# Gates behind the experts instead of in front, two experts at a time on 64 rows each, and a new order of the stages

## The chip, the core and the metric

The kernel runs on one core of a Trainium2 chip. The core has four engines that matter here: TensorE (PE, matrix products into PSUM; its weight loads are listed as PEld), VectorE (DVE), ScalarE (ACT) and GpSimd (POOL); SyncE (SP) issues the transfers. Each engine works its own instructions in program order and waits at semaphores for the others. The metric is the device time of one execution in microseconds (us), lower is better. All data are fp32.

## What is computed

The input x has 4 sequences of 4096 rows of 512. Every row goes through a mixture-of-experts network, every second row through a recurrence, and both are multiplied and added to x:

```python
xn = _layernorm(x)
# recurrence on every second row, state h of 512 x 64 per sequence
h = jnp.tanh(h * A + xt[:, :, None] * Bm);  y = h @ c_sum + Dv * xt
s = repeat(einsum(y * silu(gate), w_out) + b_out, 2)
# experts, E = 8, top 2 of 8, EH = 512, M = 64
cont = sigmoid(xn @ W_enc + b_enc) @ W_s2c + b_s2c
gate = top-2 softmax weights of cont @ Wr + br
he = relu(einsum('tm,emh->eth', cont, W1) + b1[:, None, :])
y = einsum('eth,ehm->etm', he, W2) + b2[:, None, :]
expert_out = einsum('etm,te->tm', y, gate)
g = silu(layernorm(sigmoid(expert_out @ W_c2s + b_c2s) @ W_dec + b_dec))
out = x + s * g
```

The gates are not negative. So an expert can be weighted on its input and biases (relu(g(Wc + b)) = g relu(Wc + b)) or on its output.

## The kernel before

**Blocks and steps.** The time axis is cut into 64 blocks of 32 recurrence steps. The four sequences and a half of the 64 states fill the 128 partitions; the other half of the states is a second tile, f = 1. One step is, for f = 0 and 1: VectorE multiplies h by A (`ps_z`, L1138), adds u (L1144), and ACT takes the tanh into a ring of 8 buffers `h` (L598). The order on VectorE is multiply 0, multiply 1, add 0, add 1. POOL makes u = x * B for a step (L525). PE reads four steps of h out at a time (`y`, L887, 16 instructions of 32 columns in four column groups, into `ps_y`); the tanh of every fourth step waits until the readout of the steps 8 to 5 before it is done, since it overwrites their buffers.

**The network beside it.** While block n recurs, the 256 rows of a block (two tiles q of 128) pass through: input normalisation, transposes and projection (`proj_...`), `encode`, `controller` (cont, transposed: contT), `router`, six small `route` steps and `route_gate` on VectorE, the experts, `to_spikes`, `decode`, an output layernorm (`dec_scale`, `dec_shift` on VectorE), and a last stage that joins both branches (`fin_...`). PSUM has two banks, `bank0` and `bank1`, for all of this, and `ps_acc`. A bank is filled by PE, drained by another engine, and filled again.

**The experts before.** ACT weights cont by each gate (`scale_cont`, L705 and L707, one copy of 64 columns for each expert and tile, with the gate as a 65th column), PE transposes the results (`conteT_transpose`, L959), ACT copies them (L718), and `expert_up` (L973) multiplies 65 rows, the last being the bias b1 against the gate. One call fills one bank for one half of an expert. ACT takes the relu of 512 columns (L724), `expert_down` (L985) adds 64 output rows on either half of the columns into `ps_acc`, all experts into one sum, with b2 against the transposed gates (L949, L981). `eo_fold` adds the halves (L1004). The readout is copied by ACT (`fin_y`, L666) and multiplied with the silu gate by POOL (`fin_gate`, L558).

**What sets the order.** Each engine runs the same loop over blocks in slots of a sixteenth of a step. Tables of constants at the head of the file say in which slot of its block a stage is issued on an engine: 19.9375 is behind the last instruction of step 19, numbers over 32 lie in the next block, negative ones in the one before. On VectorE the second multiply of a step is at .25 and the adds at .5 and .75; on ACT the second tanh is at .5. On PE the slots are only an order, since PE has no instruction of its own in a step. The functions `experts`, `y` and all others are called from these tables.

Of the kernel before, what the change touches and what calls it, by code (L numbers as in the profile page):

```python
# [51 lines left out]
EARLY = 16 * 12  # L52
LATE = 16 * 9
# [13 lines left out]
POOL_PROJ_SCALE = -23.875  # L70
POOL_DEC_SCALE = (31.8125, 34.6875)
POOL_FIN_SKIP = 0.4375
POOL_FIN_GATE = 36.3125
POOL_FIN_ADD = (43.375, 59.1875)
ACT_PROJ_NORM = -23.4375
ACT_PROJ_EVAC = (-22.6875, -20.25)
ACT_PROJ_SEED = (-22.3125, -9.125)
ACT_PROJ_OUT = (-20.4375, -7.25)
ACT_FIN_Y = 33.8125
ACT_Y_SEED = 5.625  # L80
ACT_SPIKES = (2.9375, 3.8125, 4.6875, 5.875)
ACT_CONTT_COPY = 6.8125
ACT_ROUTE_SIG = 9.5
ACT_SCALE_CONT = (9.9375, 10.625)
ACT_CONTET_COPY = (12.625, 12.75, 12.75, 12.9375)
ACT_GATET_COPY = 11.6875
ACT_RELU = (13.375, 13.875, 14.5625, 14.75, 15.5, 15.5625, 16.5625, 16.5625, 17.8125, 17.8125, 18.8125, 20.9375, 21.625, 21.875, 22.6875, 22.8125)
ACT_EO_COPY = 23.625
ACT_BOTH_COPY = 24.875
ACT_SPIKES_AGAIN = (25.75, 25.9375, 26.625, 27.75)  # L90
ACT_DEC_SILU = (31.5, 39.9375)
ACT_DEC_SQUARE = (29.9375, 31.625)
ACT_PROJ_SUM = (-29.25, -29.0625)
ACT_PROJ_MEAN = -28.9375
ACT_PROJ_SQUARE = (-28.0625, -27.375)
ACT_PROJ_VAR = -25.0625
ACT_FIN_EVAC = 39.875
ACT_ACC_SEED = 5.625
ACT_OUT_SEED = 38.9375
ACT_DEC_SEED = (26.3125, 27.875)  # L100
PE_Y = (19.1875, 20.375, 21.5, 34.8125, 34.9375, 37.25, 38.125, 38.375)
PE_PROJ_TRANSPOSE = (-12.0, -10.625)
PE_PROJ_IN = (-11.5625, 4.625)
PE_ENCODE = (6.4375, 7.1875, 7.3125, 11.1875)
PE_CONTROLLER = 17.125
PE_ROUTER = 19.0625
PE_CONTET = (22.0, 26.3125, 27.4375, 28.0)
PE_GATET = 21.4375
PE_EXPERTS = (28.9375, 33.3125, 34.0, 34.125, 34.4375, 34.4375, 35.5625, 35.9375, 36.25)
PE_EO_FOLD = 36.75  # L110
PE_TO_SPIKES = (36.9375, 37.3125)
PE_DECODE = (37.4375, 37.8125)
PE_FIN_TRANSPOSE = 50.8125
PE_FIN_OUT = 51.25
DVE_ROUTE = (7.75, 8.75, 9.375, 9.5, 9.625, 9.75)
DVE_ROUTE_GATE = 10.0
DVE_DEC_SCALE = (31.625, 35.8125)
DVE_DEC_SHIFT = (31.8125, 37.9375)
DVE_FIN_MUL = 42.875


def build(nc, x, w_inT, b_in, A_T, B_T, Cm, Dv, w_outT, b_out, g_norm, W_enc, b_enc, W_s2c, b_s2c,
# [12 lines left out]
    with ExitStack() as ctx:  # L135
# [17 lines left out]
        w_1 = sb("w_1", [P, E, EH])  # L153
# [6 lines left out]
        ones = sb("ones", [P, P])  # L160
# [29 lines left out]
        conte = sb("conte", [P, 2, E, MA])  # L190
        hT = sb("hT", [P, 2, 2 * T2])
# [1094 lines left out]
```

## Time and profile before

| | us |
|---|---|
| median of 3 runs | 5803.53 (5802.18 to 5803.68) |
| span of the profiled execution | 5801.0 |
| PE busy | 5580.6 |
| VectorE busy | 5403.5 |
| POOL busy | 5287.9 |
| ACT busy | 4595.4 |

The profiled execution is 2.5 us shorter than the median of the runs. Busy times count overlapped instructions once. A row of the timeline merges equal instructions that follow one another: start, time from the first start to the last end, engine, line, operation, output<-inputs, shapes, count, and in brackets the idle time before it and what ended it. Two instructions in a row on an engine overlap by their tail, so what one holds the engine is the distance of two starts, less than its own duration.

### The profile page before, as it was taken

To read this page: it belongs to the slowest core of one execution; us is meant where nothing else is said; L and a number is where in the kernel's file an instruction comes from. 1 tells how busy PE (TensorE), PEld (TensorE's weight loads), DVE (VectorE), ACT (ScalarE), POOL (GpSimd) and SP (SyncE) were. 2 spreads that over 40 slices of the span, in tenths; PEclk is the share of its full clock that TensorE was granted. 3 is DMA by queue.
4 is the path that set the end of the run, shared out by engine and by line. 5 is a ranking of instruction groups with operands and counts; after the bars stand their busy time and mean duration, and the time that the engine had idled before them with its cause. 6 is when DMAs were issued, how large, how long until landed. Compare 5 with 4: busy or idle time off the path is not lost.

```text
span 5801.0 us, 88242 instructions
## 1 busy us (share of the span) xinstructions
PE 5580.6 (96%) x28770; PEld 3073.1 (53%) x28770; DVE 5403.5 (93%) x9108; ACT 4595.4 (79%) x9941; POOL 5287.9 (91%) x2828
## 2 busy tenths in 40 slices
PE   6999999999999999999999999999999999999998
PEld 3555555555555555555555555555555555555554
DVE  5999999999999999999999999999999999999997
ACT  5878878788788787887887878878878788788786
POOL 5999999999999999999999999999999999999997
PEclk9999999999999999999999999999999999999999
DMA  6454544544444445444454454444444444444443
GB/s 166 113 121 107 122 115 111 123 112 116 120 108 121 116 111 122 112 116 120 108 120 117 110 121 113 115 120 109 119 118 110 120 114 114 120 110 118 119 109 88
DMA packets 158222, 673.41 MB, mean 116 GB/s; under 512 B 45761, under 2 KB 46785, under 8 KB 92225
## 3 DMA queue, kind: packets, MB, share of 16 engines
q1 hardware_dynamic: 157762, 667.76, 48.0%
q8 instruction: 229, 3.75, 0.3%
q14 instruction: 231, 1.89, 0.1%
HBM read 617.26 MB, written 50.33 MB: 115 GB/s over the span
## 4 chain that ended last, share of the span: by engine, by line
PE 76%; ACT 14%; DVE 7%; issue 3%; SPq 1%; DMA 0%; POOL 0%; ACTq 0%; POOLq 0%
PE bank L973 17%; PE bank L921 15%; PE ps_y L887 11%; PE ps_acc L985 9%; PE bank L1037 8%; PE ps_acc L1037 8%; ACT h L598 4%; PE bank L908 4%; DVE ps_z L1144 4%; ACT conte L707 3%; DVE ps_z L1138 2%; ACT wide L718 1%; PE bank L1020 1%; PE ps_acc L1020 1%; PE bank L959 1%
## 5 line engine op out<-in xcount | busy, mean ns | idle before, releaser
L525 POOL TENSOR_TENSOR u<-xb,bt 128x1024 f32<-128x1024 f32 x2048 | 4811.0, 2360 | 387.1 <-DVE ps_z L1144 315.6
L598 ACT ACTIVATE h<-ps_z 128x512 f32<-128x512 f32 x4096 | 2408.0, 599 | 1008.3 <-DVE ps_z L1144 807.9
L1138 DVE TENSOR_TENSOR ps_z<-h,ps_A 128x512 f32<-128x512 f32 x4096 | 2664.7, 691 | 314.7 <-ACT h L598 233.1
L1144 DVE TENSOR_TENSOR ps_z<-ps_z,u 128x512 f32<-128x512 f32 x4096 | 2655.3, 691 | 0.0
L973 PE MATMUL bank<-wide,w 65*128 65x256 f32 x4096 | 1015.0, 393 | 18.5 <-ACT wide L718 18.5
L887 PE MATMUL ps_y<-h,c_wide 128*32 128x512 f32 x8192 | 962.0, 599 | 49.0 <-ACT h L598 49.0
L921 PE MATMUL bank<-xnT,w_enc 128*128 128x256 f32 x4096 | 901.3, 381 | 2.8 <-ACT wide L671 2.8
L973 PEld LDWEIGHTS bank<-wide,w 65*128 65x128 f32 x4096 | 730.6, 189 | 315.3 <-issue 152.6
L921 PEld LDWEIGHTS bank<-xnT,w_enc 128*128 128x128 f32 x4096 | 772.9, 190 | 158.9 <-issue 53.3
L887 PEld LDWEIGHTS ps_y<-h,c_wide 128*32 128x32 f32 x8192 | 227.2, 109 | 566.8 <-issue 418.1
L908 PE MATMUL bank<-w_in,xnT 128*128 128x512 f32 x1024 | 474.4, 606 | 7.6 <-DVE c_wide L1214 1.6
L1037 PE MATMUL bank<-w_dec,wide 128*128 128x512 f32 x1024 | 456.6, 599 | 0.0
L1037 PE MATMUL ps_acc<-w_dec,wide 128*128 128x512 f32 x1024 | 449.9, 592 | 0.0
L908 PEld LDWEIGHTS bank<-w_in,xnT 128*128 128x128 f32 x1024 | 185.0, 190 | 274.0 <-issue 272.0
L1037 PEld LDWEIGHTS ps_acc<-w_dec,wide 128*128 128x128 f32 x1024 | 194.6, 190 | 244.9 <-issue 244.9
L724 ACT ACTIVATE hT<-bank 128x512 f32<-128x512 f32 x512 | 291.9, 599 | 37.3 <-PE bank L973 37.2
L1037 PEld LDWEIGHTS bank<-w_dec,wide 128*128 128x128 f32 x1024 | 189.3, 190 | 235.5 <-issue 214.6
L724 ACT ACTIVATE conte<-bank 128x512 f32<-128x512 f32 x512 | 291.2, 598 | 24.3 <-PE bank L973 24.3
L985 PE MATMUL ps_acc<-hT,w 128*64 128x256 f32 x2048 | 277.5, 392 | 0.0
L985 PE MATMUL ps_acc<-conte,w 128*64 128x256 f32 x2048 | 274.3, 389 | 0.0
L1057 PE MATMUL bank<-w_out,conte 128*128 128x512 f32 x512 | 238.5, 609 | 8.4 <-ACT conte L769 0.7
L707 ACT ACTIVATE conte<-ps_acc,gate 128x64 f32<-128x64 f32 x1024 | 228.5, 384 | 0.0
(124 smaller groups left out, 4285.1 us busy)
## 6 DMA issues: line engine op xcount, KB each, us to landing
xb<-x_proj_scratch SPq DMA_DIRECT2D x2048, 256.0 KB, 4.6
xbuf<-in_L_attn_x SPq DMA_DIRECT2D x256, 128.0 KB
xres<-in_L_attn_x SPq DMA_DIRECT2D x512, 64.0 KB
out<-g SPq DMA_DIRECT2D x256, 128.0 KB
x_proj_scratch<-xp SPq DMA_DIRECT2D x256, 64.0 KB
w_in<-in_L_attn_w_in SPq DMA_DIRECT2D x1, 2048.0 KB, 8.1
w_enc<-in_L_ffn_W_enc SPq DMA_DIRECT2D x1, 2048.0 KB, 16.5
w_dec<-in_L_ffn_W_dec SPq DMA_DIRECT2D x1, 2048.0 KB, 20.4
```

What stands on the lines that cost most here:

```text
L525: pool.tensor_tensor(u[:, tau % 2, :, :], xt, bt[:, :, :], ALU.mult).then_inc(u_ready, 1)
L598: act.activation(h[:, tau % RING, f, :], ps_z[:, f, :], ACT.Tanh).then_inc(h_ready, 1)
L707: ins = act.activation(conte[:, q, e, 0:M], cont_acc[:, q, :], ACT.Copy, scale=gate[:, q, e:e + 1])
L724: drained(act.activation(hidden[n % 4], bank[n % 2][:, :], ACT.Relu), at)
L887: ins = pe.matmul(ps_y[32 * j:32 * j + 32, :], c_wide[:, f, SP - 4 - 4 * k:2 * SP - 4 - 4 * k], h[:, (QUAD * k + j) % RING, f, :], start=F ...
L908: ins = pe.matmul(bank[half][:, :], xnT[:, par, k, 0, :], w_in[:, k, D * half:D * half + D], start=False, stop=(k == KD - 1), skip_group_c ...
L921: ins = pe.matmul(bank[n % 2][:, T2 * half:T2 * half + T2], w_enc[:, k, P * m:P * m + P], xnT[:, par, k, :, :], start=(k == 0 and half == ...
L973: ins = pe.matmul(bank[n % 2][:, T2 * half:T2 * half + T2], w_1[0:MA, e, P * t:P * t + P], conteT[:, e, :], start=(half == 0), stop=True, ...
L985: ins = pe.matmul(eo_acc[M * half:M * half + M, :], w_2[:, 4 * (n // 2) + t, :], hidden[n % 4][:, T2 * half:T2 * half + T2], start=(n == 0 ...
L1037: ins = pe.matmul(dst[:, :], wide[:, k, P * q:P * q + P], w_dec[:, k, :], start=False, stop=(k == KH - 1), skip_group_check=True)
L1138: dve.tensor_tensor(ps_z[:, f, :], h[:, (tau - 1) % RING, f, :], ps_A[:, f, :], ALU.mult).then_inc(m_done, 1)
L1144: dve.tensor_tensor(ps_z[:, f, :], ps_z[:, f, :], u[:, tau % 2, f, :], ALU.add).then_inc(z_ready, 1)
```

## The change

The gates move behind the experts. ACT no longer scales and PE no longer transposes `conte`. contT is doubled onto both halves of the partitions (`dup`, by a matmul, and `dup_copy`). `up` works two experts j = 0, 1 in one round, each on its own 64 rows and into its own bank; the bias is added in the relu, now two instructions of 256 columns. `down` sums one expert pair i in one half of `ps_acc`. The gates are spread over rows by `g_spread` (a matmul of a broadcast gate column with the identity, 128 columns, two groups of eight calls) and copied by ACT (`g_copy`). VectorE multiplies each pair with them and adds b2 (`gate_pair`), and `fold` sums four pairs. The product of the readout with the silu gate moves from ACT and POOL to VectorE (`fin_gate`). Buffers that were shared get room of their own. All slot tables are new. The router makes 64 columns instead of 128. In the prologue the two biases are loaded as rows and turned by one matmul. Bank counts are now numbered by name from the tables.

```diff
-            def scale_cont(blk, q):
...
-                for e in range(E):
-                    ins = act.activation(conte[:, q, e, 0:M], cont_acc[:, q, :], ACT.Copy,
-                                         scale=gate[:, q, e:e + 1])
...
+            def g_copy(blk, n):
+
+                wait_filled(act, f"G{n}", blk)
+                drained(act.activation(spread[:, 2 * n:2 * n + 2, :],
+                                       bank[n][:, :].rearrange("p (i t) -> p i t", i=2), ACT.Copy), f"G{n}")
...
-                drained(act.activation(hidden[n % 4], bank[n % 2][:, :], ACT.Relu), at)
...
+                for c in range(2):
+                    t = EH // P * e + 2 * (r % 2) + c
+                    ins = act.activation(hidden[:, r % 2, j, c, :], bank[j][:, T2 * c:T2 * c + T2],
+                                         ACT.Relu, bias=b_1[:, t:t + 1])
...
+            def g_spread(blk, n):
...
+                        for j in range(2):
+                            e = 2 * (2 * n + i) + j
+                            ins = pe.matmul(bank[n][M * j:M * j + M, c0:c0 + P],
+                                            gate[:, q, e:e + 1].to_broadcast([P, M]), ident[:, :],
+                                            start=(i == 0 and q == 0), stop=True, skip_group_check=True)
...
-                    ins = pe.matmul(bank[n % 2][:, T2 * half:T2 * half + T2], w_1[0:MA, e, P * t:P * t + P],
-                                    conteT[:, e, :], start=(half == 0), stop=True, skip_group_check=True)
...
+                for c in range(2):
+                    t = 2 * (r % 2) + c
+                    for j in range(2):
+                        rows = slice(M * j, M * j + M)
+                        ins = pe.matmul(bank[j][:, T2 * c:T2 * c + T2], w_1[rows, r // 2, P * t:P * t + P],
+                                        contT_both[rows, :], start=(c == 0), stop=True, skip_group_check=True)
...
+                        ins = pe.matmul(pair_acc[M * j:M * j + M, i % 2, :], w_2[:, t, :], hidden[:, r % 2, j, c, :],
...
+                for i in range(PAIRS):
+                    for j in range(2):
+                        ins = pe.matmul(eo_acc[M * j:M * j + M, :], halves, gated[:, i, :],
+                                        start=(i == 0), stop=(i == PAIRS - 1))
...
+            def gate_pair(blk, i):
+
+                dve.wait_ge(pairs_ready, 2 * blk + 1 + i // 2)
+                wait_drained(dve, f"G{i // 2}", blk)
+                dve.scalar_tensor_tensor(out=gated[:, i, :], in0=pair_acc[:, i % 2, :], scalar=b_2[:, i:i + 1],
+                                         in1=spread[:, i, :], op0=ALU.add, op1=ALU.mult).then_inc(pair_gated, 1)
+
+            def fin_gate(blk, par):
+                dve.wait_ge(y_done, NQ * (blk + 1))
+                wait_drained(dve, "GATE", blk)
+                dve.tensor_tensor(o[:, :], ps_y[:, :], gt[:, par, :], ALU.mult).then_inc(o_ready, 1)
```

The slots of which the text speaks: `DVE_GATED = (20, 19.9375, 24.375, 23.75)`, `DVE_FIN_GATE = 34.8125`, `ACT_G_COPY = (16.5, 16.5)`, and

```diff
-DVE_DEC_SHIFT = (31.8125, 37.9375)
-DVE_FIN_MUL = 42.875
+DVE_DEC_SHIFT = (33.875, 36.1875)
+DVE_FIN_MUL = 42.1875
```

On PE, the experts of the block before, in the middle of the block (rows with L887 are readouts `y`; `conte` and `hT` hold the relus):

```order
L973 MATMUL bank1<-wide,w_1 128x256 x2
L985 MATMUL ps_acc<-hT,w_2 64x256 x4
L887 MATMUL ps_y<-h,c_wide 32x512 x16
L973 MATMUL bank0<-wide,w_1 128x256 x2
L973 MATMUL bank1<-wide,w_1 128x256 x2
L985 MATMUL ps_acc<-conte,w_2 64x256 x4
```

The same engine in the changed kernel, from the readout of steps 8 to 11 (L831 is `y`, L921 `up`, L938 `down`, L904 `g_spread`):

```order
L831 MATMUL ps_y<-h,c_wide 32x512 x8
L904 MATMUL bank0<-ident,gate 64x128 x8
L904 MATMUL bank1<-ident,gate 64x128 x8
L938 MATMUL ps_acc<-hidden,w_2 64x256 x4
L921 MATMUL bank0<-contT_both,w_1 128x256
L921 MATMUL bank1<-contT_both,w_1 128x256
L921 MATMUL bank0<-contT_both,w_1 128x256
L921 MATMUL bank1<-contT_both,w_1 128x256
L938 MATMUL ps_acc<-hidden,w_2 64x256 x4
```

Two readouts stood in a row in the middle of the experts; now one stands there, the readout of steps 12 to 15, and the spreading of the gates directly behind it, ahead of the next `down` and `up`.

On ACT, steps 15 to 18 of the changed kernel (L563 is tanh, two to a step; L676 relu, L664 `g_copy`):

```order
L563 ACTIVATE h<-ps_z 128x512 x2
L676 ACTIVATE hidden<-bank0,bias_cols 128x256 x2
L676 ACTIVATE hidden<-bank1,bias_cols 128x256 x2
L563 ACTIVATE h<-ps_z 128x512 x2
L664 ACTIVATE wide<-bank0 128x512
L664 ACTIVATE wide<-bank1 128x512
L563 ACTIVATE h<-ps_z 128x512 x2
L676 ACTIVATE hidden<-bank0,bias_cols 128x256 x2
L676 ACTIVATE hidden<-bank1,bias_cols 128x256 x2
```

In the kernel before, the same steps of ACT held two relus of 512 columns between two pairs of tanh; the two copies now stand between the tanhs of step 16 and those of step 17.

On VectorE, steps 19 to 21 of the changed kernel (L1088 multiply, L1094 add, L1153 `gate_pair`):

```order
L1094 TENSOR_TENSOR ps_z<-ps_z,u 128x512 x2
L1153 SCALAR_TENSOR_TENSOR wide<-ps_acc,bias_cols,wide 128x256
L1088 TENSOR_TENSOR ps_z<-h,ps_A 128x512
L1153 SCALAR_TENSOR_TENSOR wide<-ps_acc,bias_cols,wide 128x256
L1088 TENSOR_TENSOR ps_z<-h,ps_A 128x512
L1094 TENSOR_TENSOR ps_z<-ps_z,u 128x512 x2
```

Before, nothing but the recurrence stood in these steps; now one gating stands behind the adds and the next between the two multiplies.

## Rows read from the trace of the kernel before

**Rows 1.** The page: span, busy times of the engines, chain by engine.

```profile
span 5801.0 us, 88242 instructions
...
PE 5580.6 (96%) x28770; PEld 3073.1 (53%) x28770; DVE 5403.5 (93%) x9108; ACT 4595.4 (79%) x9941; POOL 5287.9 (91%) x2828
...
PE 76%; ACT 14%; DVE 7%; issue 3%; SPq 1%; DMA 0%; POOL 0%; ACTq 0%; POOLq 0%
```

**Rows 2.** Timeline of VectorE: start us, us, engine, line, what, count, idle before.

```profile
2945.68 0.17 DVE L1158 TENSOR_SCALAR sel<-ps_acc 128x16 f32<-128x16 f32 x1
...
2963.42 1.29 DVE L1138 TENSOR_TENSOR ps_z<-h,ps_A 128x512 f32<-128x512 f32 x2
2964.62 1.29 DVE L1144 TENSOR_TENSOR ps_z<-ps_z,u 128x512 f32<-128x512 f32 x2
2965.97 1.29 DVE L1138 TENSOR_TENSOR ps_z<-h,ps_A 128x512 f32<-128x512 f32 x2
...
2976.21 1.29 DVE L1138 TENSOR_TENSOR ps_z<-h,ps_A 128x512 f32<-128x512 f32 x2
...
3007.14 0.75 DVE L1178 SCALAR_TENSOR_TENSOR bank<-bank,d_r,ln_g_all 128x512 f32<-128x512 f32 x1
3007.80 0.69 DVE L1144 TENSOR_TENSOR ps_z<-ps_z,u 128x512 f32<-128x512 f32 x1
3008.39 0.68 DVE L1187 TENSOR_TENSOR g<-bank,ln_b_all 128x512 f32<-128x512 f32 x1
3008.99 1.28 DVE L1138 TENSOR_TENSOR ps_z<-h,ps_A 128x512 f32<-128x512 f32 x2
...
3034.84 0.17 DVE L1158 TENSOR_SCALAR sel<-ps_acc 128x16 f32<-128x16 f32 x1
```

**Rows 3.** Timeline of ACT in the same block.

```profile
2965.34 1.20 ACT L598 ACTIVATE h<-ps_z 128x512 f32<-128x512 f32 x2 [0.39 <-DVE ps_z L1144]
2966.44 1.08 ACT L724 ACTIVATE hT<-bank 128x512 f32<-128x512 f32 x2
2967.90 1.19 ACT L598 ACTIVATE h<-ps_z 128x512 f32<-128x512 f32 x2 [0.39 <-DVE ps_z L1144]
...
2992.61 1.57 ACT L671 ACTIVATE wide<-bank,b_c2s_col 128x256 f32<-128x256 f32 x4
2994.05 0.61 ACT L598 ACTIVATE h<-ps_z 128x512 f32<-128x512 f32 x1
```

**Rows 4.** Waits: engine, line, waited for, us in total, times, longest.

```profile
ACT h L598 <- PE ps_y L887: 173.9, 127, 1.6
...
DVE ps_z L1138 <- ACT h L598: 233.1, 512, 2.8
```

**Rows 5.** Groups of instructions by form: busy us, mean ns, idle before.

```profile
L707 ACT ACTIVATE conte<-ps_acc,gate 128x64 f32<-128x64 f32 x1024 | 228.5, 384 | 0.0
L558 POOL TENSOR_TENSOR conte<-conte,gt 128x512 f32<-128x512 f32 x64 | 81.6, 1275 | 2.8 <-ACT conte L666 2.8
L1170 DVE SCALAR_TENSOR_TENSOR gate<-ps_acc,sel 128x16 f32<-128x16 f32 x64 | 11.1, 174 | 3.2
```

**Rows 6.** Timeline of PE in the same block.

```profile
2956.38 1.09 PE L959 MATMUL bank<-ident,conte 128*65 128x128 f32 x8
...
2966.54 1.08 PE L985 MATMUL ps_acc<-conte,w 128*64 128x256 f32 x8
2967.55 1.99 PE L973 MATMUL bank<-wide,w 65*128 65x256 f32 x8
2969.47 1.08 PE L985 MATMUL ps_acc<-hT,w 128*64 128x256 f32 x8
...
2991.44 1.13 PE L1020 MATMUL bank<-hT,w_c2s 64*128 64x256 f32 x8 [0.48 <-ACT hT L732]
2992.51 1.92 PE L887 MATMUL ps_y<-h,c_wide 128*32 128x512 f32 x16
2994.36 0.48 PE L1020 MATMUL ps_acc<-hT,w_c2s 64*128 64x256 f32 x1
```

More of the change, by code:

```diff
@@ L73 @@
[L73 to L102, printed above, removed]
@@ L977, in expert_down @@
-            def expert_down(blk, n):
-                if n == 0:
-                    pe.wait_ge(gateT_copied, blk + 1)
-                    pe.matmul(eo_acc[0:M, :], bias_2, gateT, start=True, stop=False)
-                wait_drained(pe, (blk, FILL_W1[n]))
-                for half in range(2):
-                    t = 2 * (n % 2) + half
-                    ins = pe.matmul(eo_acc[M * half:M * half + M, :], w_2[:, 4 * (n // 2) + t, :],
-                                    hidden[n % 4][:, T2 * half:T2 * half + T2],
-                                    start=(n == 0 and half == 1), stop=(n == 15))
-                if n == 15:
-                    ins.then_inc(eo_ready, 1)
@@ L991, in experts, with dup @@
-            def experts(blk, p):
-                if p < 8:
-                    expert_up(blk, 2 * p)
-                    expert_up(blk, 2 * p + 1)
-                if p > 0:
-                    expert_down(blk, 2 * p - 2)
-                    expert_down(blk, 2 * p - 1)
-            def eo_fold(blk):
-                pe.wait_ge(eo_copied, blk + 1)
-                for j in range(2):
-                    ins = pe.matmul(eo_acc[M * j:M * j + M, :], halves, eoT, start=True, stop=True)
+            def dup(blk):
+                pe.wait_ge(contT_copied, blk + 1)
+                wait_free(pe, "DUP", blk)
+                for j in range(2):
+                    ins = pe.matmul(bank[0][M * j:M * j + M, 0:T2], halves, contT[:, :], start=True, stop=True)
+                filled(ins, "DUP")
@@ new lines, in down @@
+            def down(blk, r):
+                i = r // 2
+                if r == 0:
+                    pe.wait_ge(gate_ready, blk + 1)
+                if r == ROUNDS // 2:
+                    pe.wait_ge(pair_gated, PAIRS * blk + 2)
+                for j in range(2):
+                    wait_drained(pe, f"UP{r}{j}", blk)
+                for c in range(2):
+                    for j in range(2):
+                        t = EH // P * (2 * i + j) + 2 * (r % 2) + c
+                        ins = pe.matmul(pair_acc[M * j:M * j + M, i % 2, :], w_2[:, t, :], hidden[:, r % 2, j, c, :],
+                                        start=(r % 4 == 0 and c == 0), stop=(r % 2 == 1 and c == 1),
+                                        skip_group_check=True)
+                if r % 4 == 3:
+                    ins.then_inc(pairs_ready, 1)
@@ L1021, in to_spikes @@
                                         eoT_both[rows, :], start=(half == 0), stop=True, skip_group_check=True)
-                        if half == 1 and ats[j]:
-                            filled(ins, ats[j])
+                        if half == 1 and names[j]:
+                            filled(ins, names[j])
                         elif half == 1:
@@ L1081, in _ @@
                           skip_group_check=True)
+            pe.matmul(ps_y[:, P:P + E * EH // P + PAIRS], bias_rows[:, :],
+                      ident[0:E * EH // P + PAIRS, 0:E * EH // P + PAIRS], start=False, stop=True, skip_group_check=True)
             for k in range(KH):
@@ L1247, in between @@
                         dec_shift(blk, q)
+                for i in range(PAIRS):
+                    if slot == DVE_GATED[i]:
+                        gate_pair(blk, i)
+                if slot == DVE_FIN_GATE:
+                    fin_gate(blk, par)
                 if slot == DVE_FIN_MUL:
```

436 lines of the change are left out of this document (206 added, 230 removed).

## The prediction, made before the changed kernel ran

> **What bounds the kernel now.** Read first the busy times and the chain [rows 1]. PE is busy 5580.6 of 5801.0 us, DVE 5403.5, POOL 5287.9, ACT 4595.4, and the chain names PE for 76% of the span. Three engines over 90% say little by themselves, so the second view is the one that shows which of them sets the pace: the timeline of VectorE. The gate instruction `sel` of two neighbouring blocks stands at 2945.68 and 3034.84 [rows 2]: a block of 32 steps takes 89.16 us, and 64 of them are 5706 of the 5801 us. Inside the block an undisturbed step is the distance of two pairs of multiplies: 2963.42, 2965.97, and five steps after the first 2976.21, so 2.558 us [rows 2]. A step is a closed ring. The add pair starts at 2964.62; its first add ends 0.69 later; the tanh pair starts at 2965.34 [rows 3]; the first tanh takes 0.60; the next multiply starts at 2965.97. VectorE issues four instructions of 0.60 us each (distance 3008.39 to 3008.99 of two of them) and waits 0.14 to 0.15 us for the tanh. So 32 x 2.558 = 81.85 us of a block is recurrence, and the other 89.16 - 81.85 = 7.31 us is what stands in its way.
>
> These 7.31 us have two parts. First, VectorE's own other work: 512 columns take 0.60 us of its time (`tensor_tensor`) or 0.66 (`scalar_tensor_tensor`, 3007.14 to 3007.80) [rows 2]. A piece set behind the second add hides 0.14 of it in the wait for the tanh; set anywhere else it costs all. Output scale and shift of the first half in one step 0.66 + 0.60 - 0.14 = 1.12, of the second half 0.52 and 0.46, the two final multiplies 1.20 - 0.14 = 1.06, the six small routing steps and the gate some 0.67: 3.83 us. The remainder is 7.31 - 3.83 = 3.48 us, and the waits have it: VectorE waited 233.1 us for tanh over 0.14, which is 3.64 a block [rows 4]. Behind most of that stands PE: tanh waited 173.9 us for the readout `ps_y`, which frees the ring of 8 h buffers (127 times, two a block, the longest 1.6 us) [rows 4].
>
> So VectorE's work is the floor (85.7 us a block) and PE's lateness is 3.5 us above it. The change raises the first and lowers the second.
>
> **What it does to VectorE.** It adds `gate_pair` four times (256 columns) and `fin_gate` once (512). No row has a `scalar_tensor_tensor` of 256 columns. Bounds: 16 columns took 0.174 [rows 5], 512 took 0.75 [rows 2]; the larger one holds the engine 0.66, so the issue distance is 0.09 less than the duration; on the line between both, 256 columns last 0.453 and hold it 0.36. The ends are 0.33 (half of 0.66) and 0.45 (nothing overlapped); I take 0.38, a little above the line, which rests on two far points. The Trainium skill, VectorE: DVE Perf Modes, on the TRN2 errata, has for an fp32 `tensor_tensor` (N+151)/0.96 ns, which is 424 for 256 columns; no instruction of that size is in the trace, and by it the four would hold VectorE 0.33 each. Two of the four (slots 19.9375 and 23.75) stand behind an add pair and hide 0.14 each, the others (20 and 24.375) cost all: 4 x 0.38 - 0.28 = 1.24. `fin_gate` (34.8125) stands behind an add pair: 0.60 - 0.14 = 0.46. What was there is set anew: scale 0.52 and 0.52, shift 0.46 and (36.1875, behind a first multiply) 0.60, final multiplies 1.20 (now behind a first multiply), routing 0.31, since it is spread over six steps and five of its seven pieces stand behind an add pair. Sum 3.61 + 1.24 + 0.46 = 5.31 against 3.83: **+1.48 us a block**, floor 87.16.
>
> **What it does to PE.** Before, a pair of `expert_up` (8 instructions of 65 rows) goes from 2967.55 to 2969.47, 1.92 us [rows 6]. The new one has 64 rows and alternates between two row halves and two banks. That very form is in the trace: `to_spikes` (L1020, 64 rows, 256 columns, two banks), 8 instructions from 2991.44 to 2992.51, 1.07 us [rows 6]. Eight rounds save 8 x 0.85 = 6.8 us. The transposes of `conte` go (8 instructions took 1.09, so 2.2 us for 16 [rows 6]), and smaller ones. New are the doubling of contT (4 instructions, like a quarter of a `to_spikes` pair of calls, 0.5 to 0.65), the fold over four pairs (16 instructions in two column halves; 8 such in `expert_down` take 2966.54 to 2967.55, 1.01, so 2.0 against 0.65), and the spreading of the gates: two groups of 16 instructions of 128 columns, two column halves at a time. For one group no row exists. The lower bound is half the down's 16 instructions, 1.0 us (128 columns for 256); the upper is the transposes' pace without any overlap, 16 x 1.09/8 = 2.2. `expert_down` shows that two column halves do run side by side (256 columns, 0.126 an instruction, half of the up's 0.24), so I take 1.0. PE's work falls by 6.8 + 2.2 - 0.6 - 1.35 - 2.0 = 5.0 us, from 87.2 to some 82 a block. PE stops being nearly full.
>
> **What it does to ACT and POOL.** The 16 scalings of 64 columns go (228.5 us, 3.6 a block [rows 5]), and four copies of `conteT` and the copy of ps_y. Each relu becomes two of 256 columns with a bias. The form is there: four such tanhs hold ACT from 2992.61 to 2994.05, 1.44 us, while two relus of 512 held it 1.08 [rows 3]. Between two tanh pairs ACT is free 2967.90 - 2966.44 = 1.46 us. A pair of relus now fills this to 0.02 us; before it left 0.39. POOL loses one product of 512 columns (81.6 us, 1.28 a block [rows 5]); POOL never kept VectorE waiting and had some us to spare, so nothing is taken for it. It is the cover of `fin_gate` that is gone: that work was free on POOL and is not on VectorE.
>
> **What is late next.** I walked through one block with these durations (step 16 starts at 0). The tanh of step 15 ends at 0.6; the readout of steps 12 to 15 can only then start and takes 1.85 (2992.51 to 2994.36, row of 1.92 less its tail [rows 6]), so the spreading of the gates starts at 2.5 and ends at 3.5 and 4.5, and ACT can read 0.15 later. Both `g_copy` stand in ACT's order ahead of the tanh of step 17, due at 4.49; the second runs from 4.6 to 5.1: wait 0.62. Next on PE come down(1) and up(3), whose result is readable at 6.5; two relus last until 7.9, the next tanh was due at 7.66: 0.27. Full gaps at steps 8, 19, 22, 25 and 26 cost about 0.1 each, 0.45. Together 1.34 us of waits where 3.48 were. At the block's end PE comes to the readout of steps 0 to 3 about 0.6 us before it would hold up step 8. A block is then 87.16 + 1.34 = 88.50 us, 0.66 less: 64 x 0.66 = **42 us saved**. The prologue gets two more small loads, one matmul and one copy (up to +1 us), the tail loses a copy and POOL's product (up to -1.5): nothing. 5801.0 - 42 = 5759 of span; the median of the runs is 2.5 above the span of the profiled one, so 5761.
>
> **Rivals.** (1) *The spread gates come late, slower.* Mechanism: ACT stands at the two `g_copy` in front of the tanh of step 17; each microsecond more in the two groups goes straight into the ring, since 0.62 is already exposed. At 2.2 a group instead of 1.0 the wait grows by 2.4: 90.9 a block, 5803.5 + 64 x 1.74 = 5915. The point from which it decides is +0.66 us over both groups together, 1.33 instead of 1.0 each. Against it: the side by side pairs of `expert_down`. The Trainium skill, TensorE: Matmul & The Clock Gate, Part 3, says that a weight load overlaps a running matmul only when the row group differs; both halves here have the same rows, and by that rule nothing of the group overlaps and rival 1's time results; the pace of `expert_down` speaks against it. A milder form is PE's chain from step 16 on being 1.2 us late, which after 0.6 of slack costs 0.6 and gives no change.
> (2) *The waits go altogether.* Then only VectorE's floor is left: 87.16 a block, 5803.5 - 64 x 2.0 = 5675. For it: PE has 5 us of room. Against it: ACT's gaps are full to 0.02.
> (3) *The waits do not fall.* They were not for PE's work but for its order, and the new order has as many. Then 87.16 + 3.48 = 90.64, +1.48 us a block, 5898. For it: a readout still has to wait for its four steps, and now more of ACT's work follows a product of PE closely. Against it: before, PE had two readouts in a row in the middle of the experts with the ring waiting for them; now it has one at a time, and 5 us less work.
>
> **How the numbers follow.** Forecast (5720 to 5791) 0.45, rival 2 (5665 to 5720) 0.17, no change 0.10, rivals 1 and 3 in full or in part (above 5815) 0.28. A measurement here can tell about 0.2%, 12 us, from no change. Faster 0.62, same 0.10, slower 0.28. The unknown price of `gate_pair` (0.33 to 0.45) moves the sum by -13 to +18 us, inside the forecast's own range. The range for 8 in 10 goes from 5680 to 5880; beyond it lie the full rival 1 and 3 and the last part of rival 2.
>
> **What would show it.** Two gate instructions of neighbouring blocks 88.5 us apart; undisturbed steps still 2.56; `gate_pair` holding VectorE 0.38; 8 instructions of up in 1.07 and 16 of spreading in about 1.0; VectorE's wait for tanh near 90 us instead of 233; tanh's wait for `ps_y` nearly gone. I am wrong if the spread group takes over 1.3 us, if VectorE's waits stay over 200 us, or if an undisturbed step gets longer.

## The result and the profile of the changed kernel

The changed kernel takes 5904.18 us (median of 4 runs, 5894.42 to 5913.51) against 5803.6 us of the kernel before in the same comparison: ratio 1.017, 95% interval 1.0154 to 1.0186. It is 100 us slower where 42 us less were forecast. The profiled execution spans 5905.8 us.

The page, in the order of [rows 1]: busy times, then the chain by engine.

```profile
span 5905.8 us, 92602 instructions
...
PE 5267.7 (89%) x30564; PEld 2765.4 (47%) x30564; DVE 5510.8 (93%) x9428; ACT 4532.3 (77%) x9558; POOL 5204.7 (88%) x2764
...
DVE 35%; ACT 21%; issue 15%; POOL 13%; DMA 7%; SPq 5%; PE 4%; POOLq 0%; ACTq 0%
```

PE lost 313 us of work, where 5.0 x 64 = 320 were forecast, and fell from 76% of the chain to 4%. But POOL, DMA and SyncE's queue (SPq), which had 0%, 0% and 1%, now hold 25% of it. The waits (engine, line, waited for, us in total, times, longest) say the same; L1088 and L1094 are VectorE's multiply and add, L563 is tanh, L497 POOL's product u:

```profile
POOL u L497 <- DMA xb<-x_proj_scratch: 282.4, 64, 33.9
...
DVE ps_z L1094 <- POOL u L497: 186.7, 122, 4.8
...
DVE ps_z L1088 <- ACT h L563: 41.0, 102, 2.8
```

VectorE's wait for tanh fell from 233.1 us [rows 4] to 41.0, more than forecast (90), and tanh's wait for the readout is gone. A wait that stood in no sum replaced both: 186.7 us for POOL, which stood 282.4 us for a load, 33.9 of them once, at the start. (The kernel before has only that one, 34.8 us.) The place shows in the timelines of one block. POOL (L534 is `fin_add`, output plus residual, into `g`):

```profile
3011.44 1.27 POOL L534 TENSOR_TENSOR g<-g,xres 128x512 f32<-128x512 f32 x1
3012.67 6.99 POOL L497 TENSOR_TENSOR u<-xb,bt 128x1024 f32<-128x1024 f32 x3
3022.95 7.01 POOL L497 TENSOR_TENSOR u<-xb,bt 128x1024 f32<-128x1024 f32 x3 [3.29 <-DMA xb<-x_proj_scratch]
```

SyncE's queue in the same stretch (L391 loads the residual of the second half, L408 loads a chunk of four steps of projected rows, `xb`, in 4 instructions):

```profile
3012.74 2.87 SPq L391 DMA_DIRECT2D xres<-in_L_attn_x  x4
3015.65 5.73 SPq L408 DMA_DIRECT2D xb<-x_proj_scratch  x8
```

VectorE, in that block and with its row of the block before:

```profile
2935.20 1.30 DVE L1094 TENSOR_TENSOR ps_z<-ps_z,u 128x512 f32<-128x512 f32 x2 [2.60 <-POOL u L497]
...
3025.36 1.30 DVE L1094 TENSOR_TENSOR ps_z<-ps_z,u 128x512 f32<-128x512 f32 x2 [1.95 <-POOL u L497]
```

And SyncE's queue in the kernel before, where L436 is the chunk and L419 the residual:

```profile
2938.65 47.04 SPq L436 DMA_DIRECT2D xb<-x_proj_scratch  x20
2985.74 2.85 SPq L419 DMA_DIRECT2D xres<-in_L_attn_x  x4
```

Read in order of time. POOL's addition ends at 3012.7 and frees the residual's buffer. SyncE, which had stood at that semaphore, issues the residual's four loads until 3015.6 and only then the first chunk load. POOL reaches the product of step 16 at 3019.66, the first that needs this chunk, stands 3.29 us until it has landed, and VectorE stands 1.95 us at the additions of step 16 (2.60 in the block before). In the kernel before, the residual's loads came behind all chunks of the block: the chunk's table entry was 12, the residual's 47, which is 15 of the next block. In the new one they are 13.3125 and 44, which is 12 of the next block, so the residual stands in front. The new tables also put POOL's addition one product later (44.375 for 43.375). Over the blocks the distance of two `sel` is now 90.79 us in the mean (5821.1 - 101.4 over 63), 1.63 more than 89.16. That times 64 is 104 us, which accounts for the 104.8 between the two profiled executions (5905.8 and 5801.0).

### The profile page after: what moved, and what is told of

It is laid out like the page before. It is cut to its first block, busy times and chain, and to the rows that moved or that the text cites. A ratio compares the mean times of both kernels' runs of the same rounds, so it can differ in the third digit from the quotient of the medians.

```text
span 5905.8 us, 92602 instructions
## 1 busy us (share of the span) xinstructions
PE 5267.7 (89%) x30564; PEld 2765.4 (47%) x30564; DVE 5510.8 (93%) x9428; ACT 4532.3 (77%) x9558; POOL 5204.7 (88%) x2764
## 4 chain that ended last, share of the span: by engine, by line
DVE 35%; ACT 21%; issue 15%; POOL 13%; DMA 7%; SPq 5%; PE 4%; POOLq 0%; ACTq 0%
DVE ps_z L1094 16%; DVE ps_z L1088 15%; ACT h L563 11%; POOL u L497 10%; DMA xb<-x_proj_scratch 7%; ACT hidden L676 4%; ACT wide L629 4%; SPq L391 3%; PE bank L921 2%; POOL g L534 2%; SPq L408 1%; ACT squares_p L580 1%; DVE wide L1153 1%; DVE g L1147 1%; DVE bank L1128 1%
## 5 line engine op out<-in xcount | busy, mean ns | idle before, releaser
L497 POOL TENSOR_TENSOR u<-xb,bt 128x1024 f32<-128x1024 f32 x2048 | 4806.5, 2362 | 645.0 <-DVE ps_z L1094 362.2
L563 ACT ACTIVATE h<-ps_z 128x512 f32<-128x512 f32 x4096 | 2434.2, 599 | 1164.9 <-DVE ps_z L1094 1120.5
L1094 DVE TENSOR_TENSOR ps_z<-ps_z,u 128x512 f32<-128x512 f32 x4096 | 2656.0, 692 | 186.7 <-POOL u L497 186.7
L1088 DVE TENSOR_TENSOR ps_z<-h,ps_A 128x512 f32<-128x512 f32 x4096 | 2661.8, 691 | 122.0 <-ACT h L563 41.0
L831 PE MATMUL ps_y<-h,c_wide 128*32 128x512 f32 x8192 | 988.1, 600 | 4.1 <-ACT h L563 2.0
L921 PE MATMUL bank<-contT_both,w 64*128 64x256 f32 x4096 | 593.7, 406 | 332.2 <-ACT hidden L676 194.9
L676 ACT ACTIVATE hidden<-bank,bias_cols 128x256 f32<-128x256 f32 x2048 | 809.1, 477 | 45.3 <-PE bank L921 42.4
L921 PEld LDWEIGHTS bank<-contT_both,w 64*128 64x128 f32 x4096 | 388.6, 189 | 586.6 <-ACT hidden L676 297.6
L938 PE MATMUL ps_acc<-hidden,w 128*64 128x256 f32 x4096 | 548.7, 395 | 78.6 <-DVE wide L1153 46.4
L831 PEld LDWEIGHTS ps_y<-h,c_wide 128*32 128x32 f32 x8192 | 214.0, 109 | 534.4 <-issue 414.2
L938 PEld LDWEIGHTS ps_acc<-hidden,w 128*64 128x64 f32 x4096 | 261.1, 138 | 337.0 <-issue 125.6
L1002 PE MATMUL bank<-w_out,oT 128*128 128x512 f32 x512 | 234.1, 600 | 1.3 <-ACT bank L703 1.3
L629 ACT ACTIVATE wide<-bank,b_enc_col 128x256 f32<-128x256 f32 x512 | 213.2, 471 | 1.5 <-PE bank L862 1.4
L534 POOL TENSOR_TENSOR g<-g,xres 128x512 f32<-128x512 f32 x128 | 162.6, 1271 | 12.6 <-DVE g L1146 7.5
```

What stands on the lines that cost most here:

```text
L497: pool.tensor_tensor(u[:, tau % 2, :, :], xt, bt[:, :, :], ALU.mult).then_inc(u_ready, 1)
L563: act.activation(h[:, tau % RING, f, :], ps_z[:, f, :], ACT.Tanh).then_inc(h_ready, 1)
L629: ins = act.activation(wide[:, m, :], src[:, T2 * half:T2 * half + T2], ACT.Tanh, bias=bias[:, m:m + 1], scale=0.5)
L676: ins = act.activation(hidden[:, r % 2, j, c, :], bank[j][:, T2 * c:T2 * c + T2], ACT.Relu, bias=b_1[:, t:t + 1])
L831: ins = pe.matmul(ps_y[32 * j:32 * j + 32, :], c_wide[:, f, SP - 4 - 4 * k:2 * SP - 4 - 4 * k], h[:, (QUAD * k + j) % RING, f, :], start=F ...
L921: ins = pe.matmul(bank[j][:, T2 * c:T2 * c + T2], w_1[rows, r // 2, P * t:P * t + P], contT_both[rows, :], start=(c == 0), stop=True, skip ...
```

## Experiments

Two terms serve all of them. The *block* is the mean distance of two `sel`. The *excess* of a step is how much longer than 2.557 us it takes from its first multiply to that of the next step, as the median over the blocks. Changed kernel: step 16 has an excess of 2.63 us, step 19 of 0.73.

**The order on SyncE's queue, undone.** The changed kernel with one number of a table:

```diff
-SP_RESIDUAL = (36.25, 44)
+SP_RESIDUAL = (36.25, 46)
```

> The changed kernel with one number of SyncE's table changed: the residual load of the second half tile moves from slot 44 to 46, behind the load of chunk 4 instead of in front of it. Theory A (order of SyncE's queue): in the changed kernel this load waits for POOL's fin_add, and chunk 4 stands behind it; POOL's wait for xb falls from 282 us to the 35 of the start, VectorE's wait for u from 187 us to under 15, the wait at step 17 that I had forecast (0.6 to 0.9 us a block) comes out from under it; a block is about 88.5 us and the time 5755 to 5775. Theory B (the transfers themselves are slower or collide, median landing 4.9 against 4.6 us): nothing changes in volume or number, the time stays within 15 us of 5904.

Measured: 5766.19 us (5764.87 to 5767.10), 0.9936 of before (0.9921 to 0.9951). Block 88.57 us, excess of step 16 now 0.12. The cause is shown: one entry carries 138 us. The chunk's loads no longer stand behind the residual; this is SyncE's queue:

```profile
2933.92 2.52 SPq L408 DMA_DIRECT2D xb<-x_proj_scratch  x4
2938.47 2.86 SPq L391 DMA_DIRECT2D xres<-in_L_attn_x  x4
2945.42 1.70 SPq L408 DMA_DIRECT2D xb<-x_proj_scratch  x4
```

The first row is the chunk that the product of step 16 needs. The residual of the second half follows it, issued when POOL's addition ends (2938.45 in this trace), and the third row is the next chunk. VectorE's wait for POOL is gone from the list, and what stands there instead is the wait I had forecast at 90 us:

```profile
DVE ps_z L1088 <- ACT h L563: 113.3, 328, 2.8
```

**The other member of the order.** The changed kernel with only POOL's addition at its old place:

```diff
-POOL_FIN_ADD = (44.375, 50.375)
+POOL_FIN_ADD = (43.375, 50.375)
```

> The changed kernel with the residual load where it is, but POOL's fin_add of the first half one product earlier (slot 43.375, where the kernel before had it, instead of 44.375). Theory A: the load is released 2.4 us earlier, so POOL's wait for chunk 4 falls from 3.9 to about 1.5 us a block and VectorE's wait for u from 2.9 to 0.3 to 0.8; block 88.7 to 89.3, time 5775 to 5815. Theory B: 5904 within 15 us.

Measured: 5766.57 us (5764.27 to 5769.54), 0.9937 (0.9922 to 0.9952), the same block, 88.57. The whole loss goes, more than expected. POOL still stood for chunks, 52 times, 67.6 us in all, of which 34.2 once at the start. That is little, and VectorE stood for POOL not at all:

```profile
2945.23 4.78 POOL L497 TENSOR_TENSOR u<-xb,bt 128x1024 f32<-128x1024 f32 x2 [0.53 <-DMA xb<-x_proj_scratch]
```

Two buffers of u let POOL run ahead of VectorE, and by my reading that lead took the half microsecond.

**The same order in the kernel before.**

```diff
-SP_CHUNK = (-10, 0, 9, 10, 12, 12, 12, 12)
+SP_CHUNK = (-10, 0, 9, 10, 13, 13, 13, 13)
-SP_RESIDUAL = (36, 47)
+SP_RESIDUAL = (36, 44)
-POOL_FIN_ADD = (43.375, 59.1875)
+POOL_FIN_ADD = (44.375, 59.1875)
```

> The kernel before, with the same order on SyncE: chunks 4 to 7 at slot 13 instead of 12, the second residual load at 44 instead of 47, fin_add at 44.375 instead of 43.375. Nothing of the experts is changed. Theory A: VectorE waits for u at step 16 here too, 2 to 2.9 us a block, of which up to 1 us takes the place of the waits for tanh at steps 20 to 27; block 90.8 to 91.9, time 5905 to 5975. Theory B or a cause in the new experts: 5804 within 15 us.

Measured: 5808.87 us (5802.23 to 5819.52), ratio 1.001 (1.0 to 1.0019). A clear miss: 100 to 170 us were expected, 5 came. The stall was there; POOL stood for a chunk 58 times, 217.0 us in all, 35.7 of them once at the start. These are POOL and VectorE of one block (L525 product u, L1138 and L1144 multiply and add):

```profile
2970.84 16.37 POOL L525 TENSOR_TENSOR u<-xb,bt 128x1024 f32<-128x1024 f32 x7 [4.01 <-DMA xb<-x_proj_scratch]
```

```profile
2965.36 0.69 DVE L1138 TENSOR_TENSOR ps_z<-h,ps_A 128x512 f32<-128x512 f32 x1 [0.98 <-ACT h L598]
2966.76 0.70 DVE L1138 TENSOR_TENSOR ps_z<-h,ps_A 128x512 f32<-128x512 f32 x1 [0.71 <-ACT h L598]
...
2973.23 1.30 DVE L1144 TENSOR_TENSOR ps_z<-ps_z,u 128x512 f32<-128x512 f32 x2 [0.65 <-POOL u L525]
```

Here VectorE stands 0.98 + 0.71 = 1.69 us for tanh at steps 13 and 14, just ahead of step 16, and tanh stands for PE's readout, 132.4 us in the whole run. The additions of step 16 come that much later, and the stall of 4.01 us reached VectorE as 0.65 in this block and as 10.0 us in the whole run. Medians over the blocks give the size of this cover. From the end of POOL's addition to the first multiply of step 16 lie 11.99 us in this run and 9.40 in the changed kernel. The difference of 2.59 is all of the excess of 2.63 at step 16. It has two parts. 1.60 us are, nearly all, the waits at steps 13 and 14, which the changed kernel lacks (its steps 10 to 15 take 16.83 us for 18.43). The other 0.99 has nothing to do with PE: POOL's product of step 12 waits for VectorE's additions of step 10, and the new table puts the two final multiplies ahead of these additions (`DVE_FIN_MUL` 42.1875 for 42.875), so POOL's addition ends 7.43 us behind the first multiply of step 10 instead of 6.44. So the queue's order is not dear in itself. It became dear because the same change took away what had covered it, most of it PE's lateness. This split is read from the two traces; no run changed one part alone. That leaves a prediction to test: the kernel before must lose too once the stall is larger.

**A larger stall in both kernels.** The kernel of the last experiment, and the changed kernel as it is, each with POOL's addition one product later still (45.375).

> The kernel before with the order of e3 (chunk 4's load behind the residual load on SyncE's queue, 5808.9 us) and POOL's first addition one product later still. In e3 POOL stood 4.01 us for the chunk and its lead covered all but 0.1 us a block for VectorE. My theory is that this lead is a threshold and that beyond it VectorE loses one for one: one product later is 2.3 to 2.6 us more on POOL, VectorE waits 2.1 to 2.5 us a block, block 91.3 to 91.7 us, 5930 to 5970 us. The rival, that the place of the load never matters in the kernel before (its TensorE waits take any such stall): 5803 to 5820 us.

> The changed kernel as it is, with POOL's first addition one product later (45.375 in place of 44.375). If the loss is the order on SyncE's queue (addition, then residual load, then chunk 4's load, then product 16), the addition's place sets it and VectorE, already past the threshold, loses the whole product: 2.4 to 2.6 us a block, 93.2 to 93.4 us, 6055 to 6075 us. The rival, that the chunk's transfer itself takes longer in the changed kernel (traffic, not order): the place of the addition matters little, 5895 to 5925 us.

Measured: the kernel before 6339.16 us (6326.3 to 6350.7), ratio 1.091 (1.0887 to 1.0932); the changed one 6122.72 us (6120.15 to 6123.01), 1.0536 (1.0519 to 1.0554). The rivals (no loss; traffic, not order) are out. The threshold is there: in the kernel before the first product more cost 5 us and the second 530. Both sizes were missed, though: 8.3 us a block, over three times what the product is worth, and in the changed kernel 3.4 instead of at most 2.6. In the first, 3.4 of the 8.3 stand at step 16: POOL's addition ended 3.5 us later and not 2.4, since POOL had also stood for VectorE. The rest stands at steps 18 to 20. The windows of the first one show why (start:end, length, busy time of PE, PEld, DVE, ACT, POOL with counts, then the granted clock, DMA share and GB/s):

```profile
3040.00:3045.00 5.00, 4.33 (x26) 2.41 (x24) 2.32 (x4) 1.84 (x4) 3.67 (x2) 1.00 0.95 200
3045.00:3050.00 5.00, 3.73 (x14) 2.47 (x16) 4.87 (x9) 4.31 (x9) 5.00 (x3) 0.74 0.02 3
3050.00:3055.00 5.00, 5.00 (x16) 2.86 (x16) 3.61 (x7) 2.33 (x5) 5.00 (x3) 0.50 0.73 167
```

and PE's timeline and ACT's in it:

```profile
3043.24 1.08 PE L985 MATMUL ps_acc<-hT,w 128*64 128x256 f32 x8
3046.27 2.67 PE L973 MATMUL bank<-wide,w 65*128 65x256 f32 x8 [1.95 <-ACT conte L724]
...
3050.78 3.78 PE L973 MATMUL bank<-wide,w 65*128 65x256 f32 x8
```

```profile
3059.04 1.09 ACT L598 ACTIVATE h<-ps_z 128x512 f32<-128x512 f32 x2 [4.57 <-PE ps_y L887]
```

VectorE stood 2.68 us for POOL at 3043.71; tanh and relu came late and PE stood 1.95 us. In the same 5 us the granted clock fell, and it was 0.50 over 3050 to 3055, where PE had no idle time: eight instructions of `expert_up` took 3.78 us instead of 1.92 to 1.99 [rows 6]. The readout behind them was late, tanh stood 4.57 us for it and VectorE 3.17 at the end of step 20. The clock over the whole run was 0.936 against 0.996 of the kernel before; in the changed kernel with the later addition it was 0.969, with 0.66 over 2940 to 2945. The Trainium skill, TensorE: Matmul & The Clock Gate, Part 1, describes a clock that falls from 2.4 to 1.2 GHz after idling; the trace agrees, at 0.50 and nearly twice the duration.

**The readout of steps 12 to 15 behind the next up.** In the order that the first experiment mended, five steps (17 to 20 and 22) still have an excess of 0.29 to 0.39 us. My forecast put 0.62 of waits on step 17, behind the readout.

```diff
-PE_Y = (16.25, 18.0625, 19.5, 23.3125, 34.25, ...)
+PE_Y = (16.25, 18.0625, 19.5, 24.25, 34.25, ...)
```

> The first of these runs (residual load behind chunk 4) and one number of PE's table: the readout of steps 12 to 15 moves from slot 23.3125 to 24.25, behind the spreading of the gates, down(1) and up(3). Theory A1 (the waits at steps 17 and 18 come because the spreading stands behind a readout that can only begin 0.6 us after step 16): they go, 0.9 us a block less than in the first run, time about 5705 to 5725. Rival: PE's order is tight elsewhere and ACT's gaps are full, so the wait only moves; then the time is within 12 us of the first run.

Measured: 5779.98 us (5777.72 to 5780.70), 0.9959 (0.9944 to 0.9973), 14 us slower than without this edit, a little more than the 12 us that the rival allowed. The waits at steps 17 and 18 go, and step 19 has 1.16 us instead. The wait moved, since the spreading (L904) now stands for a bank that ACT's relus hold:

```profile
2958.79 1.97 PE L904 MATMUL bank<-ident,gate 128*64 128x128 f32 x32 [0.99 <-ACT hidden L676]
```

**VectorE's own work, given back.** From here on the base is the kernel of the first experiment (5766.19 us). The final gate product goes back to a copy on ACT (slot 34.8125) and a product on POOL (36.3125).

```diff
-                if slot == DVE_FIN_GATE:
-                    fin_gate(blk, par)
...
+            def fin_y(blk):
+                act.activation(o[:, :], ps_y[:, :], ACT.Copy).then_inc(y_taken, 1)
...
+                pool.tensor_tensor(o[:, :], o[:, :], gt[:, par, :], ALU.mult).then_inc(o_ready, 1)
```

> The changed kernel with SyncE's residual load at its later place (as in the run e1, 5766.2 us, block 88.57 us), and in it the final gate product taken back from VectorE: ACT copies ps_y to SBUF and POOL multiplies it, as the kernel before does. If VectorE's own instructions count one for one on the path, as my prediction took them, the block loses the 0.44 us that the product takes behind an add pair: 88.13 us, 28 us less, about 5738 us (5730 to 5748), with ACT's and POOL's waits no longer than before. The rival, that ACT or POOL now set the pace beside VectorE: their new work (0.5 us on ACT, 1.28 us on POOL a block) comes back as waits of VectorE and the time stays at 5760 to 5775 us.

Measured: 5769.85 us (5765.19 to 5770.66), 0.9929 (0.9914 to 0.9943): no gain, so the rival holds. The excess of step 2 went from 0.43 to nothing and that of step 3 from 0.49 to 0.91. VectorE and ACT:

```profile
2998.95 0.70 DVE L1104 TENSOR_TENSOR ps_z<-h,ps_A 128x512 f32<-128x512 f32 x1 [0.31 <-ACT h L572]
```

```profile
2997.32 0.60 ACT L572 ACTIVATE h<-ps_z 128x512 f32<-128x512 f32 x1 [1.22 <-DVE ps_z L1110]
2997.81 0.62 ACT L728 ACTIVATE g<-g 128x512 f32<-128x512 f32 x1
2998.33 0.59 ACT L572 ACTIVATE h<-ps_z 128x512 f32<-128x512 f32 x1
```

ACT's SiLU (L728) stands inside the pair of tanhs and makes the second one late; VectorE's product had stood exactly beside it.

**That SiLU moved, with and without the product on VectorE.** `ACT_DEC_SILU = (34.5625, 41.1875)` for `(34.0625, 41.1875)`.

> The kernel of e5 (final gate product back on ACT and POOL, 5769.9 us, block 88.54 us) with ACT's first decoder SiLU (table entry 34.0625) moved behind the pair of tanhs it stood inside (34.5625). In e5 the 0.43 us that VectorE's product had held at step 2 was gone, but step 3 then had 0.91 us for 0.49: VectorE waited 0.31 us at 2998.95 for the second tanh half, which stood behind the SiLU (2997.81, 0.62 us) on ACT. If that SiLU is what took the gain: the wait goes and the block loses 0.3 to 0.43 us, 88.1 to 88.2 us, 5741 to 5751 us. If ACT's work of these steps as a whole is the bound (SiLU, copy of ps_y, encoder tanhs), the wait moves to the next tanh pair: 5762 to 5773 us.

> The kernel of e1 (final gate product on VectorE, SyncE's residual load later, 5766.2 us) with only that SiLU moved to 34.5625. There VectorE's product stood beside the SiLU and hid it, so no wait is there to remove: 5762 to 5770 us by my reading. Were the SiLU on the path in e1 too: 0.3 us a block less, about 5745 us.

Measured: 5761.48 us (5760.55 to 5764.01), 0.9922 (0.991 to 0.9934), with the product on POOL, and 5766.89 us (5764.64 to 5768.04), 0.993 (0.9918 to 0.9942), with it on VectorE. Moved alone it does nothing, as expected. With both, step 3 is back at 0.50, but step 8 has 0.35 that it had not: POOL, with 1.28 us more to do, is late there.

```profile
3012.06 1.30 DVE L1110 TENSOR_TENSOR ps_z<-ps_z,u 128x512 f32<-128x512 f32 x2 [0.25 <-POOL u L499]
```

Some 5 of the 28 us arrive. This is the fastest kernel of the study, 0.8% below the kernel before.

**POOL's skip product two steps earlier** (`POOL_FIN_SKIP = 0.8125` for 2.8125, on that kernel).

> The kernel of e9 (5761.5 us) with POOL's product of the skip term two steps earlier (table entry 2.8125 to 0.8125). In e9 VectorE's saved 0.43 us a block came back in part at step 8, where its additions waited 0.25 us for POOL (3012.06): POOL worked there without a wait from 2987.87 to 3018.97, now with the gate product of 1.28 us among it. Two steps earlier POOL still waits some 0.2 us a step for VectorE, so the same work fits in: if POOL's lead was what was short, the wait of 0.25 us goes, the additions of step 8 come 0.25 to 0.35 us sooner and the time is 5739 to 5747 us. If POOL as a whole is full, the wait moves to another step: 5757 to 5765 us.

Measured: 5764.03 us (5763.50 to 5765.35), 0.9928 (0.9915 to 0.9942); the wait of 0.24 us at step 8 is still there. The time lies in the range for a full POOL. I had misread the row. POOL's small waits for VectorE end one product earlier than I placed them:

```profile
2896.51 2.36 POOL L499 TENSOR_TENSOR u<-xb,bt 128x1024 f32<-128x1024 f32 x1 [0.25 <-DVE ps_z L1110]
2898.83 0.19 POOL L517 TENSOR_TENSOR d_r<-d_ss,sum_eps 128x1 f32<-128x1 f32 x1
...
2899.61 1.26 POOL L527 TENSOR_TENSOR xp<-xp,dv_all 128x512 f32<-128x512 f32 x1
```

From 2898.83 to 2930 POOL has no wait, so the product only moved inside the full stretch. A place ahead of it was not tried.

**VectorE's pieces set behind an add pair.** On the kernel of the first experiment: second scale 35.6875 to 35.8125, second shift 36.1875 to 36.8125, final products 42.1875 to 42.8125. And on the fastest kernel only the third `gate_pair`, 24.375 to 24.75.

> The run e1's kernel with three of VectorE's own pieces (second normalisation product, second shift, the final pair of products) put between a step's additions and the next step's multiplications instead of between or inside the pairs. VectorE stands some 0.15 us between the additions and the next multiplications in each step (0.16 us in the rows of e1 at 2925.5, 2928.3), and a piece put there hides that gap. If VectorE sets the pace there: 3 x 0.14 to 0.155 = 0.42 to 0.46 us a block, 27 to 30 us, about 5737 us. If it doesn't, because tanh on ACT then comes later: 5760 to 5775 us.

> The kernel of e9 with the third gate product of the expert pairs put behind the additions of its step (24.75 in place of 24.375), where the gap of 0.155 us between additions and multiplications hides part of it. No bank is held longer by more than 0.65 us. If VectorE sets the pace at steps 23 to 25 (the trace of e1 shows no wait there): 0.14 us a block, 9 us less than e9. Rival, TensorE or ACT late behind the product, as in e8: equal to e9 or slower.

Measured: 5909.27 us (5903.11 to 5909.88), ratio 1.0168 (1.0153 to 1.0183), a loss of 143 us where a gain of 27 to 30 was expected; and 5796.94 us (5794.22 to 5799.78), 0.9983 (0.9975 to 0.9992), a loss of 35 where a gain of 9 was. Both times the piece freed something for PE. In the first the three pieces were moved together, but the excess grew only at steps 10, 11 and 13, so the loss is that of the final products, which stand at step 10. What they free is a bank, for which `up` now waits (L1147 is the second of them), after PE's other waits:

```profile
3004.84 0.60 PE L841 MATMUL bank<-ident,xbuf 128*128 128x128 f32 x4
3006.24 0.65 PE L892 MATMUL bank<-contT,w_r 128*64 128x256 f32 x4 [0.80 <-ACT xnT L598]
3008.87 2.08 PE L921 MATMUL bank<-contT_both,w 64*128 64x256 f32 x8 [1.98 <-DVE g L1147]
```

The eight instructions took 2.08 us for 1.13; the windows give a granted clock of 0.84 for 3005 to 3010 and 0.82 for 3010 to 3015. Steps 11 and 13 then stood for ACT (excess 1.67 and 1.15). In the second, `fold` waited for the gated pair, 0.44 us in the block that I read; step 24 gained 0.15 (0.14 forecast), but step 25 has 0.48 of excess and step 26 0.23 where they had none and 0.04.

## Why the prediction was wrong

**The step that failed** is one clause: "POOL never kept VectorE waiting and had some us to spare, so nothing is taken for it". It is true of the kernel before and says nothing of the new one, whose tables move POOL's addition and SyncE's loads. The term that it put at nothing measured 186.7 us of VectorE's waits, an excess of 2.63 us a block at step 16. I priced VectorE, PE, ACT and POOL's work and never walked through SyncE's queue, although all its entries changed. Between a load's issue and its landing lie 4.6 to 4.9 us here, and between POOL's addition (end 3012.7) and the product that needs the chunk (3019.66) only 7.0, of which the residual's loads take 2.9. With the queue's order mended and nothing else changed the rest of the forecast comes out: 5766 measured for 5761, block 88.57 for 88.50.

**None of the three rivals was the cause.** The spreading was no slower than forecast, so rival 1 is refuted. So is, for this form, what the prediction drew from the rule of the Trainium skill beside it: in the trace of the first experiment the weight loads of a pair of matmuls start while the pair ahead, on the same rows, still runs. PE does both groups there, 32 instructions, in 1.8 us (2950.31 to 2952.10, where the next row starts; forecast 2.0; 1.80 in the changed kernel too):

```profile
2950.31 1.97 PE L904 MATMUL bank<-ident,gate 128*64 128x128 f32 x32
```

Rival 3 gave 5898 for the wrong reason. It let the waits stay at 3.48 us a block, and (186.7 + 41.0)/64 = 3.56 remained, but most of it was another wait, for POOL. Its number near the result is chance.

**Terms of the sum**, in the changed kernel:

```profile
2930.75 1.13 PE L921 MATMUL bank<-contT_both,w 64*128 64x256 f32 x8 [0.78 <-ACT hidden L676]
...
2958.51 1.95 PE L949 MATMUL ps_acc<-wide,w_r 128*64 128x256 f32 x16
```

```profile
2944.58 0.48 DVE L1153 SCALAR_TENSOR_TENSOR wide<-ps_acc,bias_cols,wide 128x256 f32<-128x256 f32 x1
2944.97 0.69 DVE L1088 TENSOR_TENSOR ps_z<-h,ps_A 128x512 f32<-128x512 f32 x1
```

Up: 1.07 forecast, and 1.13 less its tail of 0.06 measured. Fold: 2.0 and 1.95. `gate_pair` holds VectorE 0.39 (0.38 forecast; it lasts 0.48, so the 424 ns of the Trainium skill, a rule for another instruction, were too low for this one). The relus fill ACT's gap: 1.46 us from 2939.59 to 2941.05, 1.44 forecast.

**The waits left over** were 1.34 us in the forecast. In the mended kernel the view has 113.3/64 = 1.77, which counts with each wait the 0.07 or so that VectorE stands idle at the end of every step (2964.62 + 1.29 to 2965.97 [rows 2]). Above that the size is right: the steps with a wait, 16, 17, 18, 21 and 22, have an excess of 0.12 + 0.37 + 0.32 + 0.19 + 0.29 = 1.29. Their place was wrong in part, not 0.62 at one step, but small waits at five. Steps 19 and 20 lie between with 0.29 and 0.39; they hold a `gate_pair` each and no wait (forecast 0.24 and 0.38). By my reading the waits come from a chain: a pair of relus ends, PE starts the next `up` into the same banks, and ACT stands for it after its tanhs: 1.57 us of relus and 1.13 of `up`, one after the other, are more than a step of 2.56:

```profile
2953.44 1.29 DVE L1088 TENSOR_TENSOR ps_z<-h,ps_A 128x512 f32<-128x512 f32 x2 [0.44 <-ACT h L563]
...
2956.32 1.29 DVE L1088 TENSOR_TENSOR ps_z<-h,ps_A 128x512 f32<-128x512 f32 x2 [0.39 <-ACT h L563]
```

**VectorE's floor** was treated as a plain sum. The three experiments on the gate product show that it isn't: 0.43 us taken from VectorE at step 2 came back at step 3 from ACT and then at step 8 from POOL. Of the 1.48 us that the change was charged, the 0.46 for `fin_gate` would hardly have been saved by leaving it where it was. That the total of the mended kernel agreed to 0.07 us, with its waits at other steps than forecast, is partly luck.

**The range** ended at 5880; the result lies 24 us outside it. The chance of slower (0.28) had mechanisms on PE and ACT only.

## What to carry to other kernels

When a change moves a queue's table, walk through that queue as through an engine: for each load, what semaphore stands ahead of it, when that is signalled, and when the product that needs it is due. An engine that "never keeps anyone waiting" has a lead of a definite size, here at most two products of 2.3 us, the two buffers of u, and it counts as free only as long as no stall exceeds that. The lead is also eaten from the other side: POOL's product waits for VectorE's additions, and two multiplies set ahead of these took 1.0 us of it. When a change removes the largest wait, look for everything that was late behind it by less. A small instruction's place is worth more by the buffer that it frees for another engine than by the gap that it hides: moving three pieces for 0.45 us a block cost 2.2.

## What the runs showed of the hardware

- A wait stands on the issuing queue and holds every later load, also those that need nothing of it. Here it held a chunk that POOL needed, and letting the chunk pass gave 138 us. Four loads took SyncE 1.7 us (xb, 2945.42 above) to 2.9 us (xres) to issue. The Trainium skill, DMA: Bandwidth & Descriptors, Anatomy of one DMA (a section on GpSimd's DMAs), says that semaphore waits happen on the issuing sequencer before dispatch; SyncE's rows agree (residual issued at 3012.74, 0.03 us after POOL's addition, chunk 2.9 us later).
- A stall of 2 to 3 us on VectorE can cost PE its clock. Where PE stood 1.95 us, the granted clock was 0.74 in the 5 us around and 0.50, the level of 1.2 GHz, in the next 5, though PE was busy throughout these, and `up` took 3.78 us for 1.99. In the changed kernel as it is, with stalls of 2.0 to 2.6 us, the effect is small. In the block of 2935.20 PE stood 1.65 us and the clock stayed at 1.00 over 2935 to 2950; over the run it was 0.991, for 0.995 in the mended kernel, and the mean of the blocks lies only 0.13 us above their median. I had not expected it at all, since PE is busy 96% of the time in the kernel before.
- Two matmuls on the same rows and different column halves run side by side also at 128 columns: the two of a pair start 0.007 us apart and take 0.27 each, pairs start every 0.109 us, and 32 instructions take 1.8 us, 0.056 us each.
